# A graph layer on one Trainium2 core: layer 2 two blocks back and layer 1 one block back in each step, the adds directly behind the turns

## The chip, the core and the metric

The kernel runs on one core of a Trainium2 chip. The metric is the device time of one execution in microseconds (us). TensorE (PE), VectorE (DVE), ScalarE (ACT), GpSimd (POOL) and the queue of SyncE (SP), which issues DMA transfers, each run their own instructions in order and meet at semaphores.

## What is computed

```python
agg = jax.ops.segment_sum(edge_attr, dst, num_segments=6250)   # 106250 edges x 128, sorted by dst
h   = jnp.maximum(_layernorm(x, axis=-1), 0.0)                 # 6250 nodes x 128
y   = jax.nn.relu(jnp.concatenate([agg, h], axis=1) @ W1 + b1) # 256 -> 512
out = x + y @ W2 + b2                                          # 512 -> 128
```

All in float32. `src` isn't used. Each node has 17 edges on average, and the edges come sorted by their receiving node.

## The kernel before

**Tiling.** Nodes go in NB = 25 blocks of 256 (the last has 106). Edges go in rounds of 1536 (four chunks of 384), 70 rounds with the short last one; a block takes 4 (block 0), 3, or 2 (blocks 4, 10, 16 and 22) rounds, the last block takes the short one. Edge rounds land in a ring of eight slots. For each chunk DVE builds a one-hot matrix (`build`, L411) of each edge's node against a window of 32 nodes that begins at the chunk's first node, and TensorE multiplies it with the edges (`sum_rounds`, L666), which gives the sums of a window. ScalarE copies a block's sums from PSUM (`copy_sums`, L332), TensorE turns them (`turn_sums`, L677), and DVE adds each window into the node table `aggT` (`add_sums`, L481), at a place that it loads into registers from `base_tab` (L469).

**The node side.** DVE's `stats` (L424, L429), POOL's `spread` (L274 to L281) and ScalarE's `normalise` (L317) make the normalised rows `xn`; TensorE turns them (`turn_x`, L687); ScalarE rounds them into a high part (`h_out`, L324) and DVE keeps the rest as a low part (`rest_of_h`, L445). The aggregate is split in the same way by `round_agg` (ScalarE, L339) and `rest_of_agg` (DVE, L452). `layer1` (L703) has 24 products for a block, six for each quarter of the hidden units; ScalarE's `relu` (L350) brings the four quarters to SBUF, `layer2` (L715) multiplies them by W2, DVE's `finish` (L463) adds the residual with b2 (put in by `add_b2`, L438), and SP stores the block (`store`, L227).

**The order** is written out by hand: every engine runs a loop over the steps k = 0 to 24, and step k has work of several blocks. On TensorE a step is: sums of block k, layer 1 of block k-2, layer 2 of block k-3, turn of the sums of block k, turn of x of block k+1. On DVE: finish of k-4, adds of k-1, low part of h of k, one-hots of k+1, low part of the aggregate of k-1, statistics of k+2, b2 of k+1, and in steps 2, 3, 4, 5 and 7 parts of a check on whether the windows hold all edges (`overrun`, L499 to L507, and L567 to L577). On ScalarE: high part of h of k, copy of the sums of k, rounding of the aggregate of k-1, relu of k-2, normalise k+2. On SP: load of x of k+3, for each round of block k (once it is summed) a load of the round eight further, store of k-4.

Buffers that the order has to respect: one PSUM bank each for the sums, their turn, the turn of x and the output; two for the hidden units; two buffers each of `sums`, `xn`, `agg_hi`/`agg_lo`, `hidden` and `outrow`.

Of the kernel before, what the change touches and what calls it, by code (L numbers as in the profile page):

```python
# [26 lines left out]
def graph_layer(nc, x, dst, edge_attr, W1, b1, W2, b2, out):  # L27
# [40 lines left out]
    with ExitStack() as ctx:  # L68
# [137 lines left out]
        @block.sync  # L206
        def _(sp):
            def load(r):
                if r >= RING:
                    sp.wait_ge(round_summed, r - RING + 1)  # L210
                slot = r % RING
                if r == NR:
                    sp.dma_start(edges[0:KREST, slot, 0:GR * F], rest_v).then_inc(edges_landed[slot], 16)
                else:
                    sp.dma_start(edges[:, slot, :].rearrange("p (t n) -> p t n", t=TILES),  # L215
                                 rounds_v[:, r, :, :]).then_inc(edges_landed[slot], 16)

            def load_x(b):
                if b - 3 >= 4:
                    sp.wait_ge(x_landed[b % 4], 16 * ((b - 3) // 4))  # L220
                sp.dma_start(xs[:, b, :], x_v[:, b, :]).then_inc(x_landed[b % 4], 16)

            def store(n, par, b):
                sp.wait_ge(out_added, n + 1)
                w = width(b)
                if w == P:
                    sp.dma_start(out_v[:, bass.ds(b, 1), :], outrow[:, par:par + 1, :]).then_inc(stored[par], 16)  # L227
                else:
                    sp.dma_start(out_last_v, outrow[0:w, par, :]).then_inc(stored[par], 16)

            sp.dma_start(dstA[:, :], dst[0:P * CHUNK].rearrange("(c e) -> c e", e=CHUNK)).then_inc(dst_landed[0], 16)
            load(0)
            sp.dma_start(dstB[:, :], dst[P * CHUNK:2 * P * CHUNK].rearrange("(c e) -> c e", e=CHUNK)  # L233
                         ).then_inc(dst_landed[1], 16)
            sp.dma_start(dstC[:, :], dst[2 * P * CHUNK:FULL * CHUNK].rearrange("(c e) -> c e", e=CHUNK)  # L235
                         ).then_inc(dst_landed[2], 16)
            sp.dma_start(dstD[:, :], dst[FULL * CHUNK:E].rearrange("(a e) -> a e", a=1)).then_inc(dst_landed[3], 16)
            for r in range(1, RING):
                load(r)
            for k in range(NB):  # L240
                if 3 <= k + 3 < NB - 1:
                    load_x(k + 3)
                for r in ROUNDS[k]:
                    if r + RING < NROUNDS:
                        load(r + RING)
                if k >= 4:
                    store(k - 4, (k - 4) % 2, k - 4)
            for b in range(NB - 4, NB):
                store(b, b % 2, b)

            sp.wait_ge(stored[0], 16 * (NB // 2 + 1))
            sp.wait_ge(stored[1], 16 * (NB // 2))

            sp.wait_ge(flag_ready, 1)
            again = sp.value_load(flag[0:1, 0:1], min_val=0, max_val=1)
            with sp.If(again > 0):
                with sp.Fori(0, FULL) as c:
                    sp.wait_ge(wide_summed, c * NWIDE + 1)
                    sp.dma_start(edges[:, 0:1, 0:G * F], chunks_v[:, bass.ds(c, 1), :]).then_inc(wide_landed, 16)
                sp.wait_ge(wide_summed, FULL * NWIDE + 1)  # L260
                sp.dma_start(edges[0:KREST, 0, 0:GR * F], rest_v).then_inc(wide_landed, 16)
                with sp.Fori(0, NB - 1) as b:
                    store(NB + b, 0, b)
                store(2 * NB - 1, 0, NB - 1)
                sp.wait_ge(stored[0], 16 * (NB // 2 + 1 + NB))
# [37 lines left out]
        def _(act):  # L303
# [17 lines left out]
            def h_out(b):  # L321
                w = width(b)
                act.wait_ge(h_turned, b + 1)
                nc.scalar.activation(hT_hi[:, b * BLOCK:b * BLOCK + 2 * w], tr_ps[:, 0:2 * w],  # L324
                                     ACT.Copy).then_inc(hT_hi_ready, 1)
# [33 lines left out]
            nc.scalar.activation(w1_hi[:, :, :], w1[:, :, :], ACT.Copy).then_inc(w1_hi_ready, 1)  # L359
            for k in range(NB):  # L360
                h_out(k)
                copy_sums(k)
                if k == 0:
                    act.wait_ge(rel_turned, 3)
                    act.wait_ge(rel_copied, 5)
                    nc.scalar.activation(b1_col[:, :], misc_ps[:, 96:96 + HT], ACT.Copy).then_inc(b1_ready, 1)
                    act.wait_ge(b1_ready, 1)
                if k >= 1:
                    round_agg(k - 1, (k - 1) % 2, k - 1, chunks_by(k - 1))
                if k >= 2:  # L370
                    relu(k - 2, (k - 2) % 2, k - 2)
                if k + 2 < NB:
                    normalise(k + 2)
            relu(NB - 2, (NB - 2) % 2, NB - 2)
            round_agg(NB - 1, (NB - 1) % 2, NB - 1, FULL + 1)
            relu(NB - 1, (NB - 1) % 2, NB - 1)

# [15 lines left out]
        def _(dve):  # L393
# [70 lines left out]
                                        xs[0:w, bass.ds(b, 1), :].rearrange("p b f -> p (b f)"),  # L464
                                        ALU.add).then_inc(out_added, 1)

            def add_sums(k):
                first, last = (chunks_by(k - 1) if k else 0), chunks_by(k)
                _, bases = nc.values_load_multi_w_load_instructions(  # L469
                    base_tab[0:1, first:last], engines=[dve.engine], min_val=0, max_val=N - 1,  # L470
                    skip_runtime_bounds_check_because="clamped when written")
                dve.wait_ge(sums_turned, k + 1)
                if k:
                    dve.wait_ge(agg_added, first)
                order = list(range(first, last, 2)) + list(range(first + 1, last, 2))
                for n, c in enumerate(order):
                    if c == first + 1:
                        dve.wait_ge(agg_added, first + n)
                    win = aggT[:, bass.ds(bases[c - first], W)]
                    at = (c - first) * W  # L480
                    nc.vector.tensor_tensor(win, turn_ps[:, at:at + W], win, ALU.add).then_inc(agg_added, 1)  # L481
# [43 lines left out]
                                    ALU.subtract).then_inc(w1_ready, 1)  # L525

            for k in range(NB):
                if k >= 4:
                    finish(k - 4, (k - 4) % 2, k - 4)
                if k >= 1:  # L530
                    if k == 1:
                        dve.wait_ge(agg_cleared, CLEARS)
                    add_sums(k - 1)
                rest_of_h(k)
                if k == 0:
                    dve.wait_ge(rel_turned, 2)
                    turned_ab(1, rel_copied)
                    dve.wait_ge(rel_turned, 3)
                    turned_cd(rel_copied)
                    dve.wait_ge(bases_turned, 1)  # L540
                    nc.vector.tensor_scalar(base_tab[:, 0:FULL], row_ps[0:1, 0:FULL], 0.0, float(N - 1), ALU.max,
                                            ALU.min).then_inc(bases_ready, 1)
                    nc.vector.tensor_scalar(base_tab[:, FULL:FULL + 1], colD[:, 0:1], 0.0, float(N - 1), ALU.max,
                                            ALU.min).then_inc(bases_ready, 1)
                    add_b2(0)
                    dve.wait_ge(rel_copied, 5)
                    dve.wait_ge(bases_ready, 2)
                if k + 1 < NB:
                    for r in ROUNDS[k + 1]:
                        build(r)  # L550
                if k >= 1:
                    rest_of_agg(k - 1, (k - 1) % 2, k - 1)
                if k + 2 < NB:
                    stats(k + 2)
                if k + 1 < NB:
# [15 lines left out]
                if k == 7:  # L571
# [3 lines left out]
                    link(nc.vector.tensor_copy(over[:, 1:2], colD[:, 5:6]))  # L575
                    link(nc.vector.tensor_reduce(colD[:, 6:7], over[:, :], AX_X, ALU.max))
                    nc.vector.tensor_scalar(flag[:, :], colD[:, 6:7], 0.0, None, ALU.is_gt).then_inc(flag_ready, 1)  # L577
            finish(NB - 4, (NB - 4) % 2, NB - 4)
            add_sums(NB - 1)
            finish(NB - 3, (NB - 3) % 2, NB - 3)  # L580
            rest_of_agg(NB - 1, (NB - 1) % 2, NB - 1)
            finish(NB - 2, (NB - 2) % 2, NB - 2)
            finish(NB - 1, (NB - 1) % 2, NB - 1)
# [47 lines left out]
        def _(pe):  # L631
# [91 lines left out]
            for k in range(NB):  # L723
# [7 lines left out]
                    turn_cd().then_inc(rel_turned, 1)  # L731
                    turn_columns(0).then_inc(bases_turned, 1)
                if k == 2:
                    pe.wait_ge(w1_ready, 1)
                    pe.wait_ge(rel_copied, 5)
                if k >= 2:
                    layer1(k - 2, (k - 2) % 2, k - 2)
                if k == 3:
                    pe.wait_ge(w2_landed, 16)
                if k >= 3:  # L740
                    layer2(k - 3, (k - 3) % 2, k - 3)
                turn_sums(k)
                if k + 1 < NB:
                    turn_x(k + 1)
                if k == 6:
                    pe.wait_ge(overrun_ready, 4)
                    pe.wait_ge(bases_ready, 1)
                    turn_columns(5).then_inc(overrun_turned, 1)
            layer1(NB - 2, (NB - 2) % 2, NB - 2)
            layer2(NB - 3, (NB - 3) % 2, NB - 3)  # L750
            layer2(NB - 2, (NB - 2) % 2, NB - 2)
            layer1(NB - 1, (NB - 1) % 2, NB - 1)
            layer2(NB - 1, (NB - 1) % 2, NB - 1)
# [54 lines left out]
```

## Time and profile before

| | us |
|---|---|
| median of 3 runs | 219.34 (218.92 to 219.66) |
| the profiled execution: its own time | 219.65 |
| its span, first to last instruction | 217.9 |
| matmuls on TensorE (PE) | 195.5 busy, 90% |
| weight loads on TensorE (PEld) | 181.6 busy, 83% |
| DVE, ScalarE, POOL | 132.7 (61%), 92.9 (43%), 43.4 (20%) busy |
| DMA | 62.57 MB, mean 287 GB/s |

A row of groups or of the timeline has start, duration, engine, line, operation, out<-in and count; what stands in brackets is the idle time before it and what ended it. Where a row has several instructions, its duration runs from the first one's start to the last one's end. The end of a matmul is modelled. A step of the chain of waits is what the end of the program hung on at that time. TensorE's granted clock is given as a share of its full speed.

### The profile page before, as it was taken

The numbers are of one execution on the slowest core, as the hardware profiler recorded it, in microseconds if no ns is written. First come the engines' busy times: TensorE is split into PE (matmuls) and PEld (weight loads), VectorE is DVE, ScalarE is ACT, GpSimd is POOL, SyncE is SP. The second block draws the span as 40 slices with busy tenths as digits, with TensorE's granted clock in tenths as the row PEclk, the third lists the DMA queues.
The fourth block names the chain that finished last, engine by engine and source line by source line (L and its number), as shares of the span: only waits on it lengthen the run. The fifth ranks groups of instructions, "written<-read, shape, count | busy, mean of one in ns | idle before, by whom it ended". The sixth has DMA issues, their size and how long they took to land.

```text
span 217.9 us, 7403 instructions
## 1 busy us (share of the span) xinstructions
PE 195.5 (90%) x2813; PEld 181.6 (83%) x2813; DVE 132.7 (61%) x590; ACT 92.9 (43%) x229; POOL 43.4 (20%) x120
## 2 busy tenths in 40 slices
PE   1326959999999999999999999999999999999990
PEld 0214749999999999999999999999999999999880
DVE  2532777788888886477656764775578458531110
ACT  2230034454343664545445445455545464533320
POOL 4464012220222102222022022211220221100000
PEclk9999988999999999999999999999999999999997
DMA  6999999999999999998999999989999910000100
GB/s 212 296 371 371 376 374 377 377 377 375 380 383 384 385 385 373 380 367 277 333 382 342 328 346 375 354 255 346 379 339 346 347 32 24 27 24 20 34 24 13
DMA packets 44768, 62.57 MB, mean 287 GB/s; under 512 B 1939, under 2 KB 44438, under 8 KB 44732
## 3 DMA queue, kind: packets, MB, share of 16 engines
q1 hardware_dynamic: 43326, 60.78, 80.0%
q10 hardware_dynamic: 1406, 1.30, 1.9%
q8 instruction: 23, 0.38, 0.7%
q14 instruction: 13, 0.11, 0.1%
HBM read 58.88 MB, written 3.20 MB: 285 GB/s over the span
## 4 chain that ended last, share of the span: by engine, by line
PE 85%; DMA 7%; DVE 2%; issue 2%; SPq 1%; DVEq 0%
PE bank L703 35%; PE bank L666 21%; PE bank L715 21%; DMA edges<-in_edge_attr 7%; PE bank L677 4%; PE bank L687 2%; PE bank L659 1%; DVE aggT L481 1%; DVE onehot L411 1%; SPq L215 1%; DVE outrow L463 0%; PE bank L634 0%; SPq L233 0%; PE bank L645 0%; SPq L235 0%
## 5 line engine op out<-in xcount | busy, mean ns | idle before, releaser
L666 PE MATMUL bank<-edges,onehot 128*32 128x128 f32 x1656 | 55.7, 290 | 6.2 <-DMA edges<-in_edge_attr 6.2
L666 PEld LDWEIGHTS bank<-edges,onehot 128*32 128x32 f32 x1656 | 47.3, 117 | 12.4 <-DMA edges<-in_edge_attr 7.6
L350 ACT ACTIVATE hidden<-bank,b_col 128x256 f32<-128x256 f32 (+1 forms) x100 | 41.0, 466 | 30.6 <-PE bank L703 30.5
L715 PE MATMUL bank<-w,hidden 128*128 128x128 f32 (+1 forms) x400 | 48.9, 275 | 0.5 <-DVE outrow L463 0.5
L481 DVE TENSOR_TENSOR aggT<-bank,aggT 128x32 f32 x277 | 36.5, 192 | 20.0 <-issue 16.7
L715 PEld LDWEIGHTS bank<-w,hidden 128*128 128x128 f32 (+1 forms) x400 | 46.5, 189 | 1.0 <-DVE outrow L463 0.7
L317 ACT ACTIVATE xn<-xs,shift,rstd 128x128 f32<-128x128 f32 (+1 forms) x50 | 22.0, 486 | 44.5 <-POOL shift L281 44.5
L463 DVE TENSOR_TENSOR outrow<-bank,xs 128x256 f32<-128x256 f32 (+1 forms) x25 | 10.6, 424 | 40.3 <-PE bank L715 40.3
L274 POOL TENSOR_SCALAR var<-meanvar 128x2 f32<-128x2 f32 (+1 forms) x25 | 7.4, 297 | 135.8 <-DVE meanvar L429 135.8
L411 DVE TENSOR_TENSOR onehot<-relT,iota 128x384 f32<-128x384 f32 x69 | 34.3, 550 | 0.3 <-ACT iota L355 0.3
L703 PE MATMUL bank<-hT_hi,w_hi 128*128 128x256 f32 (+1 forms) x100 | 30.7, 307 | 0.0
L703 PE MATMUL bank<-agg_lo,w_hi 128*128 128x256 f32 (+1 forms) x100 | 28.5, 285 | 0.0
L703 PE MATMUL bank<-hT_lo,w_hi 128*128 128x256 f32 (+1 forms) x100 | 28.3, 283 | 0.0
L703 PE MATMUL bank<-agg_hi,w_lo 128*128 128x256 f32 (+1 forms) x100 | 28.1, 281 | 0.0
L703 PE MATMUL bank<-agg_hi,w_hi 128*128 128x256 f32 (+1 forms) x100 | 27.9, 279 | 0.0
L703 PE MATMUL bank<-hT_hi,w_lo 128*128 128x256 f32 (+1 forms) x100 | 27.8, 278 | 0.0
L332 ACT ACTIVATE sums<-bank 128x384 f32<-128x384 f32 (+3 forms) x25 | 11.6, 465 | 26.3 <-PE bank L666 24.9
L703 PEld LDWEIGHTS bank<-hT_hi,w_hi 128*128 128x128 f32 x100 | 18.8, 188 | 4.6 <-issue 4.6
L703 PEld LDWEIGHTS bank<-hT_lo,w_hi 128*128 128x128 f32 x100 | 19.0, 190 | 0.0
L703 PEld LDWEIGHTS bank<-hT_hi,w_lo 128*128 128x128 f32 x100 | 19.0, 190 | 0.0
L703 PEld LDWEIGHTS bank<-agg_hi,w_lo 128*128 128x128 f32 x100 | 18.8, 188 | 0.0
L703 PEld LDWEIGHTS bank<-agg_hi,w_hi 128*128 128x128 f32 x100 | 18.8, 188 | 0.0
(90 smaller groups left out, 189.1 us busy)
## 6 DMA issues: line engine op xcount, KB each, us to landing
edges<-in_edge_attr SPq DMA_DIRECT2D x69, 768.0 KB, 9.0
out_rows<-outrow SPq DMA_DIRECT2D x24, 128.0 KB, 8.5
xs<-in_x SPq DMA_DIRECT2D x21, 128.0 KB, 8.1
w<-in_L_gnn_W ACTq DMA_DIRECT2D x1, 512.0 KB, 6.6
xs<-in_x ACTq DMA_DIRECT2D x1, 384.0 KB, 3.9
hidden<-in_dst SPq DMA_DIRECT2D x2, 192.0 KB, 5.8
w<-in_L_gnn_W ACTq DMA_DIRECT2D x1, 256.0 KB, 10.2
edges<-in_edge_attr SPq DMA_DIRECT2D x1, 133.0 KB
```

Of the source, the lines that this page charges most:

```text
L274: nc.gpsimd.tensor_scalar(var[0:w, par, :], meanvar[0:w, par, :, 1], 1e-5, None, ALU.add).then_inc(var_ready, 1)
L317: ins = nc.scalar.activation(xn[0:w, par, j, :], xs[0:w, b, j * F:(j + 1) * F], ACT.Relu, bias=shift[0:w, par, j:j + 1], scale=rstd[0:w, p ...
L332: nc.scalar.activation(sums[0:rows, k % 2, 0:n], sums_ps[0:rows, 0:n], ACT.Copy).then_inc(sums_copied, 1)
L350: nc.scalar.activation(hidden[par][:, t, 0:2 * w], hid_ps[t // 2][:, (t % 2) * 2 * w:(t % 2 + 1) * 2 * w], ACT.Relu, bias=b1_col[:, t:t + ...
L411: nc.vector.tensor_tensor(hot, of.unsqueeze(2).to_broadcast([p, n, W]), iota[0:p, 0:W].unsqueeze(1).to_broadcast([p, n, W]), ALU.is_equal) ...
L463: nc.vector.tensor_tensor(outrow[0:w, par, :], out_ps[0:w, 0:2 * F], xs[0:w, bass.ds(b, 1), :].rearrange("p b f -> p (b f)"), ALU.add).the ...
L481: nc.vector.tensor_tensor(win, turn_ps[:, at:at + W], win, ALU.add).then_inc(agg_added, 1)
L666: ins = nc.tensor.matmul(sums_ps[t * W:(t + 1) * W, cols], onehot[:, hots, e, :], edges[:, slot, e * F:(e + 1) * F], start=(g == 0), stop= ...
L677: ins = nc.tensor.transpose(turn_ps[:, i * F:i * F + rows], sums[0:rows, k % 2, i * F:(i + 1) * F], ident[0:rows, 0:rows])
L687: ins = nc.tensor.transpose(tr_ps[:, j * w:(j + 1) * w], xn[0:w, par, j, :], ident[0:w, 0:w])
L703: ins = nc.tensor.matmul(o, wt[:, half, cols], v, start=(i == 0), stop=(i == 5))
L715: ins = nc.tensor.matmul(out_ps[0:w, j * F:(j + 1) * F], hidden[par][:, t, j * w:(j + 1) * w], w2[:, t, :], start=(t == 0), stop=(t == HT ...
```

## The change

No instruction is added or taken away. In step k TensorE now has: sums of block k, **layer 2 of block k-2**, the two turns, **layer 1 of block k-1**. On ScalarE the rounding of the aggregate of k-1 stands ahead of the copy of the sums of k, and the relu is that of block k-1 and comes last, behind normalise. On DVE the low part of the aggregate comes ahead of the one-hots, and the step ends with: loading the windows' places, finish of k-2, adds of k (before, the adds of k-1 came in step k, behind finish of k-4). SP stores block k-3 in step k.

```diff
-                if k >= 4:
-                    store(k - 4, (k - 4) % 2, k - 4)
-            for b in range(NB - 4, NB):
+                if k >= 3:
+                    store(k - 3, (k - 3) % 2, k - 3)
+            for b in range(NB - 3, NB):
                 store(b, b % 2, b)
...
             for k in range(NB):
                 h_out(k)
+                if k >= 1:
+                    round_agg(k - 1, (k - 1) % 2, k - 1, chunks_by(k - 1))
                 copy_sums(k)
...
-                if k >= 1:
-                    round_agg(k - 1, (k - 1) % 2, k - 1, chunks_by(k - 1))
-                if k >= 2:
-                    relu(k - 2, (k - 2) % 2, k - 2)
                 if k + 2 < NB:
                     normalise(k + 2)
-            relu(NB - 2, (NB - 2) % 2, NB - 2)
+                if k >= 1:
+                    relu(k - 1, (k - 1) % 2, k - 1)
...
             for k in range(NB):
-                if k >= 4:
-                    finish(k - 4, (k - 4) % 2, k - 4)
-                if k >= 1:
-                    if k == 1:
-                        dve.wait_ge(agg_cleared, CLEARS)
-                    add_sums(k - 1)
                 rest_of_h(k)
...
+                if k >= 1:
+                    rest_of_agg(k - 1, (k - 1) % 2, k - 1)
                 if k + 1 < NB:
                     for r in ROUNDS[k + 1]:
                         build(r)
-                if k >= 1:
-                    rest_of_agg(k - 1, (k - 1) % 2, k - 1)
...
-            finish(NB - 4, (NB - 4) % 2, NB - 4)
-            add_sums(NB - 1)
-            finish(NB - 3, (NB - 3) % 2, NB - 3)
+                bases = load_bases(k)
+                if k >= 2:
+                    finish(k - 2, (k - 2) % 2, k - 2)
+                if k == 0:
+                    dve.wait_ge(agg_cleared, CLEARS)
+                add_sums(k, bases)
...
                 if k == 2:
-                    pe.wait_ge(w1_ready, 1)
-                    pe.wait_ge(rel_copied, 5)
+                    pe.wait_ge(w2_landed, 16)
                 if k >= 2:
-                    layer1(k - 2, (k - 2) % 2, k - 2)
-                if k == 3:
-                    pe.wait_ge(w2_landed, 16)
-                if k >= 3:
-                    layer2(k - 3, (k - 3) % 2, k - 3)
+                    layer2(k - 2, (k - 2) % 2, k - 2)
                 turn_sums(k)
                 if k + 1 < NB:
                     turn_x(k + 1)
...
-            layer1(NB - 2, (NB - 2) % 2, NB - 2)
-            layer2(NB - 3, (NB - 3) % 2, NB - 3)
+                if k == 1:
+                    pe.wait_ge(w1_ready, 1)
+                    pe.wait_ge(rel_copied, 5)
+                if k >= 1:
+                    layer1(k - 1, (k - 1) % 2, k - 1)
             layer2(NB - 2, (NB - 2) % 2, NB - 2)
```

ScalarE, steps 1 and 2, from the turn of x of block 1 on (`agg_hi` is the aggregate's high part, `hidden` the relu's output), before:

```order
L324 ACTIVATE hT_hi<-bank 128x256
L332 ACTIVATE sums<-bank 128x384
L339 ACTIVATE agg_hi<-aggT 128x256
L317 ACTIVATE xn<-xs,shift,rstd 128x128 x2
L324 ACTIVATE hT_hi<-bank 128x256
L332 ACTIVATE sums<-bank 128x384
L339 ACTIVATE agg_hi<-aggT 128x256
L350 ACTIVATE hidden<-bank,b_col 128x256 x4
L317 ACTIVATE xn<-xs,shift,rstd 128x128 x2
```

and with the change:

```order
L324 ACTIVATE hT_hi<-bank 128x256
L339 ACTIVATE agg_hi<-aggT 128x256
L332 ACTIVATE sums<-bank 128x384
L317 ACTIVATE xn<-xs,shift,rstd 128x128 x2
L350 ACTIVATE hidden<-bank,b_col 128x256 x4
L324 ACTIVATE hT_hi<-bank 128x256
L339 ACTIVATE agg_hi<-aggT 128x256
L332 ACTIVATE sums<-bank 128x384
L317 ACTIVATE xn<-xs,shift,rstd 128x128 x2
L350 ACTIVATE hidden<-bank,b_col 128x256 x4
```

The copy of the sums went behind the rounding, and the relu behind normalise, a step earlier than it was.

TensorE, the end of step 1, all of step 2 and the start of step 3. Before:

```order
L677 MATMUL bank<-ident,sums 128x128 x3
L687 MATMUL bank<-ident,xn 128x128 x2
L666 MATMUL bank<-edges,onehot 32x128 x36
L703 MATMUL bank<-hT_hi,w_hi 128x256
...
L703 MATMUL bank<-agg_hi,w_lo 128x256
L677 MATMUL bank<-ident,sums 128x128 x3
L687 MATMUL bank<-ident,xn 128x128 x2
L666 MATMUL bank<-edges,onehot 32x128 x36
```

and with the change:

```order
L677 MATMUL bank<-ident,sums 128x128 x3
L687 MATMUL bank<-ident,xn 128x128 x2
L703 MATMUL bank<-hT_hi,w_hi 128x256
...
L703 MATMUL bank<-agg_hi,w_lo 128x256
L666 MATMUL bank<-edges,onehot 32x128 x36
L715 MATMUL bank<-w,hidden 128x128 x8
L677 MATMUL bank<-ident,sums 128x128 x3
L687 MATMUL bank<-ident,xn 128x128 x2
```

Layer 1 of block 0 (24 products) now comes ahead of the sums of block 2, and layer 2 of block 0 comes a step earlier, between sums and turns.

## Rows read from the trace of the kernel before

**Rows 1.** Who TensorE waited for: us in total, times, longest

```profile
PE bank L666 <- DMA edges<-in_edge_attr: 6.2, 3, 3.5
PE bank L677 <- DVE aggT L481: 2.3, 1, 2.3
```

**Rows 2.** Chain that ended last, a step of three rounds, then sums of two

```profile
149.20 2.10 PE bank L666 x72
151.30 3.06 PE bank L703 x24
154.37 1.78 PE bank L715 x16
156.15 0.33 PE bank L677 x3
156.48 0.22 PE bank L687 x2
...
179.19 1.45 PE bank L666 x48
```

**Rows 3.** Timeline, all engines, around the adds of block 0

```profile
29.45 0.48 ACT L332 ACTIVATE sums<-bank 128x384 f32<-128x384 f32 x1
29.62 0.90 DVE L481 TENSOR_TENSOR aggT<-bank,aggT 128x32 f32 x7 [0.36 <-issue]
...
30.55 0.44 ACT L339 ACTIVATE agg_hi<-aggT 128x256 fp32r<-128x256 f32 x1 [0.62 <-DVE aggT L481]
...
30.66 0.73 PE L677 MATMUL bank<-ident,sums 128*128 128x128 f32 x3 [2.33 <-DVE aggT L481]
```

**Rows 4.** Stretches of 1 us, TensorE: length, PE busy, clock share, DMA, GB/s

```profile
30.00:31.00 1.00, 0.34 (x3) 0.91 1.07 375
...
34.00:35.00 1.00, 1.00 (x36) 0.88 1.06 387
```

**Rows 5.** Timeline of DVE in steps 5 to 7

```profile
54.22 0.53 DVE L499 TENSOR_REDUCE colC<-relC 20x1 f32<-20x384 f32 x1
...
57.13 0.43 DVE L463 TENSOR_TENSOR outrow<-bank,xs 128x256 f32<-128x256 f32 x1
58.05 1.22 DVE L481 TENSOR_TENSOR aggT<-bank,aggT 128x32 f32 x8 [0.49 <-issue]
...
63.41 0.42 DVE L463 TENSOR_TENSOR outrow<-bank,xs 128x256 f32<-128x256 f32 x1
...
66.10 0.41 DVE L445 TENSOR_TENSOR hT_lo<-bank,hT_hi 128x256 fp32r<-128x256 f32 x1
...
68.75 0.25 DVE L429 BATCH_NORM_AGGREGATE meanvar<-halves 128x2 f32<-128x6 f32 x2
...
69.23 0.42 DVE L463 TENSOR_TENSOR outrow<-bank,xs 128x256 f32<-128x256 f32 x1
```

**Rows 6.** Timeline of ScalarE in steps 3 and 7

```profile
44.17 1.56 ACT L350 ACTIVATE hidden<-bank,b_col 128x256 f32<-128x256 f32 x4
...
70.80 0.88 ACT L317 ACTIVATE xn<-xs,shift,rstd 128x128 f32<-128x128 f32 x2 [2.67 <-POOL shift L281]
71.58 0.36 ACT L324 ACTIVATE hT_hi<-bank 128x256 fp32r<-128x256 f32 x1
```

**Rows 7.** Timeline, all engines, the last layers

```profile
203.22 0.84 ACT L350 ACTIVATE hidden<-bank,b_col 128x256 f32<-128x256 f32 x2 [0.59 <-PE bank L703]
...
205.00 0.42 DVE L463 TENSOR_TENSOR outrow<-bank,xs 128x256 f32<-128x256 f32 x1 [4.29 <-PE bank L715]
...
205.48 2.05 PE L715 MATMUL bank<-w,hidden 128*128 128x128 f32 x16 [0.52 <-DVE outrow L463]
```

**Rows 8.** Transfers that read the tile outrow

```profile
DMA to landing us min/median/max: 1.7/8.5/10.3
```

**Rows 9.** Line L279, the power on POOL: ns min/median/max, first and last start

```profile
L279 POOL TENSOR_TENSOR rstd<-var,power x25: 702/709/875, 6.2 to 185.0; 128x2 f32<-128x2 f32 x24, 53x2 f32<-53x2 f32 x1
```

More of the change, by code:

```diff
@@ L465, in finish, with load_bases @@
                                         ALU.add).then_inc(out_added, 1)
-            def add_sums(k):
+            def load_bases(k):
                 first, last = (chunks_by(k - 1) if k else 0), chunks_by(k)
@@ L471, in add_sums @@
                     skip_runtime_bounds_check_because="clamped when written")
+                return bases
+            def add_sums(k, bases):
+                first, last = (chunks_by(k - 1) if k else 0), chunks_by(k)
                 dve.wait_ge(sums_turned, k + 1)
```

## The prediction

> **What bounds the kernel now.** I read the waits of TensorE first: the largest are 6.2 us for edges, all before 20 us, and 2.3 us in front of the turn of a block's sums, at 28.3 to 30.7 [rows 1, 3]. Behind that only 0.5 us is left, at 205 [rows 7]. In between the chain of waits is one unbroken row of TensorE work: a step is 2.10 (sums) + 3.06 (layer 1) + 1.78 (layer 2) + 0.33 + 0.22 (turns) = 7.49 us [rows 2], and no other engine appears in it. So an order of the same work can move the time only in three places: where TensorE starts to run without a gap, where its tail has a gap, and where the new order makes a gap that was not there. Nothing is removed or added: counts per engine are the same.
>
> **The start.** Up to the adds of block 0 both programs have the same order on every engine. Those adds end at 29.62 + 0.90 = 30.52 us [rows 3]. Before, the copy of block 1's sums (L332) was done at 29.45 + 0.48 = 29.93, so the turn L677 started at 30.66, behind the adds alone. Now ScalarE has the rounding of block 0's aggregate (L339, waits for those adds) ahead of that copy. L339 starts at 30.55 and takes 0.44; an activation begins some 0.08 to 0.1 before the end of the one ahead of it, as L324 at 71.58 does behind xn [rows 6], so the copy starts at 30.91 and with its 0.48 ends at 31.39. With the 0.07 to 0.1 us that a hand-over takes here (30.52 to 30.63), the turn starts at 31.45 instead of 30.66: **+0.8 us**. Layer 1 of block 0 follows at once (its low part is ready at 31.05 + 0.4 = 31.45 on DVE), and the sums of block 2 behind it find their one-hots built; so +0.8 is the whole shift.
>
> The clock softens this. The granted share is 0.91 over the slice 30 to 31 and 0.88 over 34 to 35, and it was 0.50 between [rows 4]: TensorE, idle for 2.3 us, fell to the lower level (1.2 of 2.4 GHz) at about 30.9 and rose again at about 34.3. If fall and rise stay where they are, the later restart spends 0.8 us less of the slow stretch working, at half speed: -0.4 us. If the stretch moves along with the restart, 0. The stretch began while TensorE was idle, so I take the first: start = **+0.4**, bounds +0.4 and +0.8. A second slow stretch of the same 3.4 us would cost 1.7 more; it is part of the upper range.
>
> **The steps.** I put t = 0 at the start of a step's sums. TensorE: sums to 2.10, layer 2 to 3.88, turns to 4.43, layer 1 to 7.49. What must be ready, with the durations of [rows 5, 6]:
> - ScalarE applies the second half of layer 1's relu behind layer 1 (0.07 + 0.84 us, as at 203.22 [rows 7]): done at 8.4, which is 0.9 of the next step. Layer 2 of that block wants it at 2.10: margin 1.2.
> - The turn of h's block (L324) follows on ScalarE at 0.8, DVE's L445 0.39 later (0.36 and a hand-over of 0.03), then L339 and DVE's L452, done by 2.1. Layer 1 wants it at 4.43: margin 2.3.
> - The copy of the sums is done at 2.10 + 0.5 = 2.6 and wanted at 3.88.
> - DVE from L445 to the end of the statistics takes 69.00 - 66.10 = 2.90 us whatever the order of the four items in it, so they end at 4.1; finish follows behind layer 2 and the adds end near 6.9. Next needed: 8.3.
>
> The narrow place is a **ring through four engines**. The relu now stands behind normalise, which waits for POOL, which waits for DVE's statistics, which wait for L324, which stands behind the previous relu. Its length: L324 to L445 0.39, DVE 2.90, statistics to xn 1.80 (69.00 to 70.80), xn to the next activation 0.78 (70.80 to 71.58), four relus 1.46 (1.56 less the 0.1 by which the next one overlaps). Sum 7.33 us against TensorE's 7.49. It fits, by 0.16 us. With only two rounds in a block both get shorter by 0.5 to 0.7. I therefore put the steady steps at **0**.
>
> DVE's own round is 69.23 - 63.41 = 5.82 us a step [rows 5], 1.67 less than TensorE's. In step 4 it has 57.13 - 54.22 = 2.91 us of overrun checks besides, now ahead of finish and the adds. With layer 1 of block 0 from 32.5 to 36.8 (most of it at the slow clock), the sums of blocks 2 to 6 start at 36.8, 44.3, 51.8, 58.5 (behind a step of two rounds) and 66.0. In step 4 L324 starts at 52.6, the statistics end at 55.9 (two rounds built in step 3, three here), L438 lets go at 56.1, the checks at 59.1, loading eight window bases takes 58.05 - 57.13 - 0.34 = 0.58, finish 0.34, eight adds 1.2: they end at 61.2. L339 and the copy of block 5's sums are done at 62.1. TensorE comes out of block 5's sums at 60.6 and out of layer 2 of block 3 at 62.4, and wants the copy there: margin 0.3. The next statistics end 3.1 us behind those adds, at 64.3; xn starts at 66.1, the relus of block 4 at 66.9, and the fourth is done at 68.5. Layer 2 starts at 68.1 and its fourth product wants it at 68.8: margin 0.3 again. Then the ring gains 0.16 a step. I take **0**, with bounds 0 and 1.6, the 2.91 less the spare 1.3 us between adds (6.9) and L445 (8.2 to 8.7) of a quiet step.
>
> The junctions of TensorE's work are new: sums to layer 2, turns to layer 1, layer 1 to sums. In [rows 2] a change into or out of the sums costs some 0.1 us of exposed weight load each way (72 records of sums take 2.10 where 48 take 1.45, so 1.95 and 0.15 for the edges), and both changes stay, one in and one out per step. I take 0; bounds 0.1 us either way in each of 22 steps, so -2.2 and +2.2.
>
> The queues: SP's store of a block moves one step forward and its loads wait for the sums of blocks that now run some 5 us later. A store lands 8.5 us after its issue, at most 10.3 [rows 8]. Store k-4 is issued at about 2.6 of step k-1 and finish k-2, the first to reuse that buffer, comes at 4.9 of step k: 9.8 us later. A landing of 10.3 delays finish by 0.5, and the adds have 1.4 to spare. Loads are eight rounds ahead, 20 us, and land in 9. Cost 0. The later sums also mean that SP waits more for TensorE and less for full queues; nobody waits for that.
>
> POOL: the page "GPSIMD Engine Reference" of the Trainium skill (section Specifications) says that GpSimd shares its interfaces to SBUF with VectorE and contends with DVE instructions that have two SBUF inputs. Here L438 is one, and it runs into POOL's first small operation in both orders. The power on POOL takes 702 to 875 ns, 709 in the middle [rows 9], so the trace shows 0.17 us at most. By that rule the ring could be 7.5 rather than 7.33; by the rows it is not, and the sum goes by the rows.
>
> **The tail.** Before, layer 2 of block 23 followed that of block 22 and waited for its finish: 205.00 to 205.48 [rows 7], 0.48 us. Now layer 1 of block 23 lies in front of it, so finish 22 is long done; but its own relu is not. Two products fill 0.45 us, the third relu is ready after 0.07 + 0.47 and the fourth after 0.91, where the products want them at 0.45 and 0.67: 0.26 us lost with the hand-over. -0.48 + 0.26 = **-0.2**. The last layer 1 wants L452 of block 24, ready 1.4 us after layer 1 of block 23, and gets there after 2.0.
>
> **Sum.** +0.4 + 0 + 0 - 0.2 = +0.2 us on the profiled execution's own 219.65: 219.85, say **219.9**. That execution stands 0.3 above the median of the runs shown, 219.34. I keep 219.9 for the median too: a run that escapes the slow stretch is what I suspect behind the lowest, 218.92, and a gap of 3.1 us instead of 2.3 makes that rarer.
>
> **The rivals.** A measurement of this kernel can tell 0.3%, 0.66 us, from no change.
> - *The checks in step 4 open a gap* (other side: slower). Finish and adds of block 4 behind 2.91 us of checks, then L339, then the copy, then TensorE. It decides as soon as the chain is 0.3 us longer than I summed. Price up to 1.6: 219.9 + 1.6 = 221.5, in the middle 220.7. For it: two margins of 0.3 built from some fifteen durations. Against: 1.67 us of slack a step.
> - *The ring is longer than TensorE's step* (slower). From 7.49 on it decides; at 7.65 it costs 0.16 in each of some 18 steps: 2.9 us, 222.8. The skill's rule on shared interfaces would be such a cause. Against it: each piece was read while DVE and POOL ran side by side.
> - *The junctions are cheaper* (faster): layer 2 right behind the sums loads its weights under them. 0.1 x 22 = 2.2: 217.7. The rows give no sign, since the load is exposed at every entry to and exit from the sums.
> - *Nothing to be seen*: start and tail cancel: 219.3 to 219.6. It is the low end of my own case.
>
> **How the numbers follow.** My forecast, steps without a gap and 219.3 to 220.4: 0.62, of which two thirds stay within 0.66 us of the median. Gap in steps 4 to 6: 0.2. Ring: 0.1. Junctions faster: 0.08. So faster 0.08, within 0.3% 0.50, slower 0.42. The range leaves out the cheap junctions and most of the long ring: 219.1 to 221.8.
>
> **What would show it.** Right: TensorE's first turn after the idle gap starts at 31.4 to 31.5; the chain has steps of 7.49 without a wait; layer 2 of block 23 shows a short wait for L350 and none for L463; ScalarE's xn waits for POOL less than now. Wrong: waits of TensorE for L332 or L350 near 62 and 68 us (first rival), waits for L350 in many steps and a step over 7.5 (second), a step under 7.45 (third), or TensorE waiting for edges.

## The result and the profile after

The changed kernel takes 220.82 us in the median of 12 runs (220.37 to 222.27), the kernel before 219.27 (218.78 to 219.66, 12 runs beside them): a ratio of 1.0074, 95% interval 1.0056 to 1.0091. It is slower by 1.55 us, inside the range, and more than the 0.6 us that was forecast. The profiled execution took 220.76 us with a span of 219.0, against 219.65 and 217.9 before: 1.1 us more. Where that 1.1 us lies can be read from the two traces. Of all the runs in this document one is left out of a median and a ratio: a run of the kernel before with ten added matmuls took 291.22 us at a mean granted share of 0.684.

TensorE's waits in the changed kernel, us in total, times, longest (before: [rows 1]):

```profile
PE bank L666 <- DMA edges<-in_edge_attr: 6.1, 3, 3.3
...
PE bank L677 <- ACT sums L332: 3.0, 1, 3.0
PE bank L715 <- DVE outrow L462: 0.4, 1, 0.4
```

The turn now waits for ScalarE's copy and not for the adds. And the wait of layer 2 for finish is there still, but no longer at the end: it is at 60 us.

**Start.** The timeline around the adds of block 0, where [rows 3] stand before:

```profile
29.90 0.43 DVE L484 TENSOR_TENSOR aggT<-bank,aggT 128x32 f32 x3
30.25 0.41 DVE L444 TENSOR_TENSOR hT_lo<-bank,hT_hi 128x256 fp32r<-128x256 f32 x1
30.36 0.43 ACT L339 ACTIVATE agg_hi<-aggT 128x256 fp32r<-128x256 f32 x1 [1.05 <-DVE aggT L484]
30.70 0.47 ACT L332 ACTIVATE sums<-bank 128x384 f32<-128x384 f32 x1
...
31.23 0.69 PE L677 MATMUL bank<-ident,sums 128*128 128x128 f32 x2 [2.95 <-ACT sums L332]
```

The adds end at 29.90 + 0.43 = 30.33 us, 0.2 earlier than before, and the turn starts 0.90 us behind them, where it was 0.14: a shift of 0.76 us against the 0.8 that was summed. The clock's slices of 1 us answer to [rows 4]:

```profile
30.00:31.00 1.00, 0.00 (x0) 0.97 1.07 378
34.00:35.00 1.00, 1.00 (x9) 0.83 1.06 389
```

With 0.97 and 0.83 the lower level reaches from some 30.9 to 34.3, as before. It stayed where it was and TensorE worked less of it, but by 0.2 us and not by 0.4, since TensorE also began 0.2 us earlier than I had put it.

**A step** of three rounds in the chain of waits, in the new order (before: [rows 2]):

```profile
149.64 1.98 PE bank L715 x16
151.62 0.33 PE bank L677 x3
151.95 0.22 PE bank L687 x2
152.17 2.86 PE bank L703 x24
155.03 2.10 PE bank L666 x72
```

1.98 + 0.33 + 0.22 + 2.86 + 2.10 = 7.49 us, the sum of before. Layer 2 has 0.2 more and layer 1 has 0.2 less: what the engine loses on the way out of the sums now stands in front of layer 2. The junctions cost the same.

**Block 3, at 60 us.** Here the chain leaves TensorE:

```profile
58.91 0.15 DVE colD L505
...
59.27 0.15 DVE colD L510
59.41 0.47 DVEq L468
...
60.03 0.43 DVE outrow L462
60.47 0.04 issue
60.51 2.05 PE bank L715 x16
```

Checks, loading of the windows' places, finish of block 2, and only then layer 2 of block 3. The sums of block 5 take 2.61 us from their first product to the next line's, where other steps have 2.10: a gap of 0.51. In layer 2 of block 3, in the turns behind it and in the next layer 2 another 0.14 us go. Together 0.65 us.

DVE was not made late by step 4 alone. Between the adds of block 0 and 60.51 us this chain holds no instruction of TensorE. After one pass over POOL and ScalarE in step 1 it runs in a loop over the low part of the aggregate, one-hots, statistics, b2, checks, loading of the places, adds, and ScalarE's rounding in between, and the checks of steps 2 and 3 are in it as well:

```profile
41.04 0.47 DVE colA L502
...
42.69 0.70 DVEq L468
...
48.35 0.47 DVE colB L502
...
49.99 0.71 DVEq L468
```

The low part of the aggregate (L451) starts at 38.16, 45.94, 53.63 and 62.03 us, so DVE's rounds of steps 2, 3 and 4 take 7.78, 7.69 and 8.40 us. The sums start at 36.17, 43.67, 51.17 and 57.90, so TensorE has steps of 7.50, 7.50 and 6.73 us there.

**Tail**, as the chain has it:

```profile
203.08 0.17 PE bank L677
203.25 3.09 PE bank L703 x24
206.34 0.02 issue
206.36 0.48 ACT hidden L350
...
206.89 1.75 PE bank L715 x12
208.64 2.62 PE bank L703 x24
211.26 1.99 PE bank L715 x16
```

Layer 2 waits for its own relu, and not for a finish as in [rows 7]. From the turn at 203.08 to the end of the last layer 2 at 213.25 it is 10.17 us. Before, the same stretch took 12.20 us (199.94 to 212.14) with one layer 2 (1.78) more in it, so 10.42 without. The tail gains 0.25 us.

So the profiled execution has -0.2 (adds earlier) + 0.76 - 0.2 (clock) + 0.65 - 0.25 = +0.8 of its +1.1. Of the other 0.3 us some 0.2 lie in step 6, where three turns of the checks now stand between the turn of x and layer 1; the rest I can't place. This is TensorE's own account. It does not say that the start, put back alone, would return its part, since the chain at 60 us comes from DVE.

### The profile page after: what moved, and what is told of

The parts are those of the page before. It is cut to its first block, busy times and chain, and to the rows that moved or that the text cites. A ratio compares the mean times of both kernels' runs of the same rounds, so it can differ in the third digit from the quotient of the medians.

```text
span 219.0 us, 7403 instructions
## 1 busy us (share of the span) xinstructions
PE 196.2 (90%) x2813; PEld 182.6 (83%) x2813; DVE 131.2 (60%) x590; ACT 87.8 (40%) x229; POOL 43.4 (20%) x120
## 4 chain that ended last, share of the span: by engine, by line
PE 71%; DVE 11%; DMA 7%; issue 3%; ACT 2%; SPq 1%; DVEq 1%; POOL 1%; POOLq 0%
PE bank L703 28%; PE bank L715 20%; PE bank L666 17%; DMA edges<-in_edge_attr 7%; DVE onehot L410 3%; PE bank L677 3%; PE bank L687 2%; DVE aggT L484 2%; DVE halves L423 1%; DVEq L468 1%; ACT hidden L350 1%; PE bank L659 1%; DVE agg_lo L451 1%; SPq L215 1%; ACT agg_hi L339 1%
## 5 line engine op out<-in xcount | busy, mean ns | idle before, releaser
L666 PE MATMUL bank<-edges,onehot 128*32 128x128 f32 x1656 | 54.7, 287 | 6.1 <-DMA edges<-in_edge_attr 6.1
L666 PEld LDWEIGHTS bank<-edges,onehot 128*32 128x32 f32 x1656 | 46.5, 115 | 11.6 <-DMA edges<-in_edge_attr 7.8
L715 PE MATMUL bank<-w,hidden 128*128 128x128 f32 (+1 forms) x400 | 51.7, 282 | 0.6 <-DVE outrow L462 0.4
L350 ACT ACTIVATE hidden<-bank,b_col 128x256 f32<-128x256 f32 (+1 forms) x100 | 38.7, 458 | 12.7 <-PE bank L703 12.7
L484 DVE TENSOR_TENSOR aggT<-bank,aggT 128x32 f32 x277 | 34.4, 187 | 6.3 <-issue 2.2
L274 POOL TENSOR_SCALAR var<-meanvar 128x2 f32<-128x2 f32 (+1 forms) x25 | 7.4, 296 | 140.6 <-DVE meanvar L428 140.6
L410 DVE TENSOR_TENSOR onehot<-relT,iota 128x384 f32<-128x384 f32 x69 | 34.3, 551 | 0.5 <-ACT iota L355 0.5
L444 DVE TENSOR_TENSOR hT_lo<-bank,hT_hi 128x256 fp32r<-128x256 f32 (+1 forms) x25 | 10.4, 416 | 33.0 <-ACT hT_hi L324 33.0
L703 PEld LDWEIGHTS bank<-agg_lo,w_hi 128*128 128x128 f32 x100 | 19.0, 190 | 0.0
```

Of the source, the lines that this page charges most:

```text
L274: nc.gpsimd.tensor_scalar(var[0:w, par, :], meanvar[0:w, par, :, 1], 1e-5, None, ALU.add).then_inc(var_ready, 1)
L350: nc.scalar.activation(hidden[par][:, t, 0:2 * w], hid_ps[t // 2][:, (t % 2) * 2 * w:(t % 2 + 1) * 2 * w], ACT.Relu, bias=b1_col[:, t:t + ...
L410: nc.vector.tensor_tensor(hot, of.unsqueeze(2).to_broadcast([p, n, W]), iota[0:p, 0:W].unsqueeze(1).to_broadcast([p, n, W]), ALU.is_equal) ...
L444: nc.vector.tensor_tensor(hT_lo[:, cols], tr_ps[:, 0:2 * w], hT_hi[:, cols].bitcast(F32), ALU.subtract).then_inc(hT_lo_ready, 1)
L666: ins = nc.tensor.matmul(sums_ps[t * W:(t + 1) * W, cols], onehot[:, hots, e, :], edges[:, slot, e * F:(e + 1) * F], start=(g == 0), stop= ...
L703: ins = nc.tensor.matmul(o, wt[:, half, cols], v, start=(i == 0), stop=(i == 5))
```

## The experiments

The theory after reading the traces: the start costs a copy (0.76 less what the clock gives back), the checks cost 0.65, everything else is level. Rivals: the ring through POOL and the relu, or the junctions. Four kernels undo parts of the change. In all diffs lines are those of the changed kernel.

**Copy first, in step 1 alone**

```diff
                 h_out(k)
+                if k == 1:
+                    copy_sums(k)
                 if k >= 1:
                     round_agg(k - 1, (k - 1) % 2, k - 1, chunks_by(k - 1))
-                copy_sums(k)
+                if k != 1:
+                    copy_sums(k)
```

> The changed kernel (220.8 us) with one thing put back: in step 1 alone the copy of the sums (L332) stands ahead of the rounding of the aggregate (L339) again. Theory (the start costs a copy behind the adds): the first turn starts some 0.1 us behind the adds again and not 0.9, TensorE works 0.75 us more of the slow stretch at half speed, so 0.75 less 0.4 comes back: 220.4 to 220.5. But TensorE then reaches block 5 some 0.4 us earlier, where DVE is not earlier, and if the gap in front of layer 2 of block 3 hangs on DVE alone it grows by what the start gained: then 220.8 as before. Rival (the start is nothing, the time is in the gap at 60 us): 220.8 too, but with the gap unchanged at 0.5. The trace tells the two apart.

Measured: 221.0 us (220.5 to 221.19), ratio 1.0075 (1.0055 to 1.0094). Nothing is won. Two of the waits of its TensorE:

```profile
PE bank L680 <- DVE aggT L487: 1.6, 1, 1.6
PE bank L718 <- DVE outrow L465: 0.7, 1, 0.7
```

The turn waits for the adds again, and the wait for finish has grown from 0.4 to 0.7. From the first product of block 5's sums to layer 2 it is 2.88 us and not 2.61, so the gap grew from 0.51 to 0.78 us. DVE reaches block 3 when it does, and a TensorE that comes earlier waits longer. In the profiled execution the slow stretch also fell later, onto layer 1 of block 0 in full (granted share 0.50 from 31.95 to 35.36 us).

**Checks later**

```diff
-                if k == 2:
+                if k == 10:
                     dve.wait_ge(limit_ready, 1)
                     overrun(colA, relA, limit[:, 0:1])
-                if k == 3:
+                if k == 12:
                     overrun(colB, relB, limit[:, 1:2])
-                if k == 4:
+                if k == 14:
                     overrun(colC, relC, limit[0:CC, 2:3])
+                if k == 16:
                     overrun(colD, relD, None)
-                if k == 5:
+                if k == 17:
...
-                if k == 7:
+                if k == 19:
...
-                if k == 6:
+                if k == 17:
                     pe.wait_ge(overrun_ready, 4)
```

> The changed kernel with the checks of the windows moved from steps 2, 3, 4, 5, 7 to 10, 12, 14, 16, 17, 19, the last two parts apart. Theory (the gap in front of layer 2 of block 3 and the small ones behind it, 0.65 us in the trace, come from the checks that stand ahead of finish and adds): no wait of TensorE for L462 near 60 us, 220.2. Rival (the ring DVE, POOL, ScalarE is too long by itself): the gap comes a few steps later and the time stays at 220.8.

Measured: 220.2 us (218.65 to 220.47), ratio 1.0023 (1.0000 to 1.0046). These are all the waits of its TensorE:

```profile
PE bank L667 <- DMA edges<-in_edge_attr: 6.2, 3, 3.4
PE bank L635 <- DVE relA L489: 4.1, 1, 4.1
PE bank L688 <- ACT xn L317: 3.3, 1, 3.3
PE bank L678 <- ACT sums L332: 2.6, 1, 2.6
```

No wait for finish is left, and none came up later. The checks cost 0.6 us.

**Both edits**

> Both edits. Theory: start and gap add up, 220.8 - 0.65 - 0.4 = 219.8, or 0.3 less if the tail's gain shows; within 0.5 of the kernel before. If it stays over 220.5, something else than start and gap makes the new order slower (junctions of TensorE's work).

Measured: 219.6 us (218.36 to 220.26, 12 runs), ratio 1.0003 (0.9985 to 1.0021): level with the kernel before. With the gap gone, the start seems worth the 0.6 us that it wasn't worth alone: that is the difference of the two medians, and the intervals of the two ratios, 1.0000 to 1.0046 and 0.9985 to 1.0021, overlap. Together the two parts account for all of the measured loss. The profiled execution, 220.26 us, is the longest of the twelve, and its clock shows why (length of the slice, PE busy, granted share, DMA):

```profile
29.00:30.00 1.00, 0.00 (x0) 0.66 1.06 373
30.00:31.00 1.00, 0.90 (x5) 0.50 1.06 372
...
35.00:36.00 1.00, 1.00 (x7) 0.50 1.06 375
36.00:37.00 1.00, 1.00 (x27) 0.92 1.09 382
```

Here TensorE ran at the lower level for 6.8 us and not 3.4, though it was busy from 30.1 on.

**Finish ahead of the checks, in step 4 alone**

```diff
                 if k == 4:
+                    finish(k - 2, (k - 2) % 2, k - 2)
                     overrun(colC, relC, limit[0:CC, 2:3])
...
-                if k >= 2:
+                if k >= 2 and k != 4:
                     finish(k - 2, (k - 2) % 2, k - 2)
```

> The changed kernel, in step 4 alone finish of block 2 ahead of the checks; the adds stay behind them. Theory A (TensorE waits for finish, and nothing stands close behind): the gap at 60 us goes, 220.3. Theory B (the adds and the copy of block 5's sums are nearly as late): the gap of 0.5 is replaced by one of 0.1 to 0.4 in front of the turn of block 5's sums, 220.5 to 220.7.

Measured: 221.4 us (220.87 to 222.33), ratio 1.0105 (1.0081 to 1.0128). Theory B, and more than it said; three of the six runs, 221.54 to 222.33 us, have a mean granted share of 0.979 to 0.980, the others 0.990 to 0.995. TensorE and DVE there:

```profile
59.75 2.05 PE L716 MATMUL bank<-w,hidden 128*128 128x128 f32 x16
62.39 0.44 PE L678 MATMUL bank<-ident,sums 128*128 128x128 f32 x2 [0.59 <-ACT sums L332]
```

```profile
59.45 0.15 DVE L510 SCALAR_TENSOR_TENSOR colD<-colD 1x1 f32<-1x1 f32 x1
60.28 1.22 DVE L484 TENSOR_TENSOR aggT<-bank,aggT 128x32 f32 x8 [0.68 <-issue]
```

Layer 2 starts at once, but the turn behind it waits 0.59 us for the copy and starts at 62.39, where it started at 62.42. The adds start at 60.28 and not at 60.37, but DVE's statistics (L428) ended 0.31 us earlier in this execution; from there to the adds it takes 0.22 us longer. From L510 to the first add it is 0.83 us, and 1.10 with finish in between, so there finish costs 0.27 us. Ahead of the checks it costs 0.50: from the start of b2 (L437) to that of the first check (L502) it is 0.81 us, and 0.31 without it. So two hand-overs lay within a few tenths of each other, finish to layer 2 and adds to copy to turn, and both hang on the checks.

**The slow stretch.** Ten matmuls that nothing reads fill TensorE's idle time, in the kernel before and in the changed one with both edits:

```diff
                 turn_sums(k)
...
+                if k == 1:
+                    for i in range(10):
+                        nc.tensor.matmul(out_ps[:, 0:F], ident[:, :], ident[:, :], start=True, stop=True)
                 turn_sums(k)
```

> The kernel before with ten 128x128 matmuls of the identity with itself into the output's bank, behind the sums of block 1, where TensorE has nothing to do for 2.3 us; nothing reads them. Theory (the slow stretch at 31 to 34 us comes from that idle time and costs what the trace shows, 1.6 us): the granted share stays at 1.0 and the time falls from 219.3 to 217.7. Rival (the clock falls anyway, or the time is won back nowhere because another engine is just as late): 219.3.

Measured: 218.84 us (218.09 to 219.62, 11 runs) against 219.27, ratio 0.9987 (0.9973 to 1.0001). That is a quarter of what was expected, and the interval still holds no change. The clock stays at 1.00 in all slices from 28 to 34 us, but a new wait appears:

```profile
38.66 0.86 PE L666 MATMUL bank<-edges,onehot 128*32 128x128 f32 x24 [0.25 <-DMA edges<-in_edge_attr]
```

In the order of before the sums of block 3 now run ahead of their edges; the sums of that block take 0.46 us longer. The old order needs the edges early, and DMA already moved 370 to 375 GB/s in the slices from 28 to 34 us. That is 0.5 of the missing 1.2 us. The profiled execution itself is 1.1 us shorter than that of before (218.52 against 219.65), as theory and edge wait together would have it.

The runs of the kernel before say that 1.6 us was too high a price for the median. A full stretch of 3.41 us at half clock takes 3.41 / 2 / 217.9 = 0.008 off the mean granted share. Of the 55 runs of before that were taken beside the experiments, six have a share of 0.998 or 0.999 and so had no such stretch. Their median is 219.05 us, that of the other 49, with 0.981 to 0.992, is 219.35. So the old order gains some 0.3 us when the stretch stays away, whether or not the ten matmuls see to it. With both edits in the new order it is more: the two runs with a share of 0.993, which is too high for a full stretch, took 218.36 and 218.39 us, the other ten 219.05 to 220.26. Why the old order gains only 0.3 is not shown beyond the edge wait.

> The changed kernel with copy first in step 1, checks later, and the same ten matmuls. Theory: 219.8 - 1.5 = 218.3, or a bit less. With layer 1 of block 0 at full speed TensorE comes 1.4 us earlier to every later block while DVE, POOL and ScalarE are not earlier; if the ring then binds, part of it is lost in the steps behind: 218.3 to 219.5.

Measured: 218.47 us (218.24 to 218.83), ratio 0.9965 (0.9953 to 0.9978), faster than the kernel before. Layer 1 and layer 2 of block 0 now stand between the sums of blocks 1, 2 and 3, and TensorE's waits behind 22 us hold none for edges. It loses 0.33 us in front of layer 2 of block 0, where the relu waits for xn.

**The ring.** One more operation of 0.47 us on DVE in each step from 8 on, in both kernels:

```diff
+                if k >= 8:
+                    nc.vector.tensor_tensor(relA[:, :].rearrange("p (e w) -> p e w", w=W),
...
                 if k + 2 < NB:
                     stats(k + 2)
```

> The kernel before with one more DVE operation of 0.47 us in each step from 8 on, ahead of the statistics; it writes a tile that only the branch for windows that hold not all edges would read, and that branch isn't taken. DVE's round is 5.82 + 0.47 = 6.29 us against TensorE's 7.49: 219.3, no change.

Measured: 219.29 us against 219.27, ratio 1.0000 (0.9986 to 1.0013). No change.

> The changed kernel with the same operation. If the ring L324, DVE, POOL, xn, relu, L324 is 7.33 us long, it is 7.80 now, and over the 16 steps it falls 5.8 us behind TensorE's own pace, of which 1 us is spare: 225 to 226, with waits for L350 or L317 in most steps. If the ring isn't closed (DVE's load alone counts, 6.29 us a step): 220.8.

Measured: 225.57 us (225.02 to 226.51), ratio 1.0302 (1.0279 to 1.0325), 4.8 us over the changed kernel, as the ring has it. ScalarE's timeline in it shows the ring turn:

```profile
103.63 0.88 ACT L317 ACTIVATE xn<-xs,shift,rstd 128x128 f32<-128x128 f32 x2 [4.61 <-POOL shift L281]
104.42 1.54 ACT L350 ACTIVATE hidden<-bank,b_col 128x256 f32<-128x256 f32 x4
105.84 0.39 ACT L324 ACTIVATE hT_hi<-bank 128x256 fp32r<-128x256 f32 x1
...
113.65 0.39 ACT L324 ACTIVATE hT_hi<-bank 128x256 fp32r<-128x256 f32 x1
...
121.45 0.39 ACT L324 ACTIVATE hT_hi<-bank 128x256 fp32r<-128x256 f32 x1
```

L324 follows L324 after 7.81 and 7.80 us: 7.33 + 0.47. The relu has no idle time in front of it, it follows xn directly, and xn waits 4.6 us for POOL. In its trace layer 2 takes 0.3 us more in nearly every step.

The same kernel, with the relu ahead of normalise:

```diff
+                if k >= 1:
+                    relu(k - 1, (k - 1) % 2, k - 1)
                 if k + 2 < NB:
                     normalise(k + 2)
-                if k >= 1:
-                    relu(k - 1, (k - 1) % 2, k - 1)
```

> The changed kernel with the additional DVE operation of 0.47 us in each step from 8 on, as in the run before (225.6 us), but on ScalarE the relu of block k-1 stands ahead of normalise k+2. The operation writes a tile that only the branch not taken would read. Theory (the ring runs through xn and relu): the relu no longer waits for POOL, the ring is L324, DVE, POOL, xn, L324 and 1.46 us shorter, 6.3 us with the operation, and nothing is lost from it: 220.8, or up to 0.5 less. Rival (DVE's load or its hand-overs as such): 225.6 again.

Measured: 221.78 us (219.64 to 222.5), ratio 1.0122 (1.0097 to 1.0148). 3.8 of the 4.8 us are gone: the ring ran through xn and relu. ScalarE now waits for TensorE and not for POOL. The wait for POOL is 12.3 us in all, where the changed kernel has 94.0:

```profile
ACT hidden L350 <- PE bank L707: 94.4, 50, 3.7
ACT xn L317 <- POOL shift L281: 12.3, 3, 5.7
```

**The relu ahead of normalise, alone**

> The changed kernel with the relu ahead of normalise, nothing else. The gap in front of layer 2 of block 3 hangs on DVE's checks and finish. L324 comes 0.8 us later in a quiet step, but in steps 3 and 4 xn was late itself. Theory: the checks still fall on the same place, 220.8, gap 0.3 to 0.6. If the gap goes, the ring had a share in it: the statistics of step 4 then end earlier: 220.2.

Measured: 221.28 us (219.79 to 221.77), ratio 1.0088 (1.0056 to 1.0119). The gap at 60 us grew to 0.9 us, more than I had expected at most. It is the same 0.9 in the run before, which explains the 1 us that stayed there. L324, now behind normalise too, starts at 37.70 us in step 2 and not at 37.40, DVE's L444 behind it at 38.10 and not at 37.82, and DVE's loop over the checks carries that on: finish of block 2 starts at 60.36 and not at 60.03. In steps 3 and 4 DVE no longer waits for L324. So the relu's place does not cure the gap; it trades the ring for a later DVE.

**All together:** copy first, checks later, ten matmuls, relu ahead of normalise.

> Copy first in step 1, checks later, ten matmuls in the idle time (218.5 us together), and the relu ahead of normalise. The 0.3 us that TensorE lost in front of layer 2 of block 0 at 36 us, where the relu waited for xn, go: 218.2. If normalise, now behind the relu, makes the next turn of x late: 218.5 or more.

Measured: 218.24 us (217.98 to 218.58), ratio 0.9954 (0.9935 to 0.9972): the fastest of all, 1.1 us under the kernel before (219.36 beside it). From the first turn to the tail TensorE waits for nobody; the start of its chain there:

```profile
28.74 2.48 PE bank L743 x20
31.22 0.33 PE bank L681 x3
31.55 0.22 PE bank L691 x2
31.77 2.87 PE bank L707 x24
34.64 2.10 PE bank L670 x72
36.74 1.98 PE bank L719 x16
```

L743 are the ten matmuls in the idle time (the trace has two records for each); layer 2 of block 0 follows the sums of block 2 without a gap.

## Why the prediction was right and wrong

- *TensorE bounds every step, and the order changes nothing in it.* Right: 7.49 us in both, junctions included.
- *Start +0.4, bounds 0.4 and 0.8.* The shift was 0.76 (0.8 summed), shown by the hand-over in the trace and by the pair of experiments (0.6 us between checks later alone and both edits). The clock gave back 0.2 and not 0.4, so the value lay between my bounds. My reason for the choice was misread: in [rows 3, 4] the share of 0.91 puts the fall at 30.8 us, and TensorE had begun again at 30.66, so the stretch did not begin while it was idle. That it stayed in its place in the profiled execution is luck as far as these runs show; in those of "copy first" and "both edits" it began at 31.95 and 29.32. And in the changed kernel as it stands the start is not on the chain of waits, since DVE's loop holds up layer 2 at 60 us either way.
- *Steps 4 to 6: 0, with two margins of 0.3 and a bound of 1.6.* This is the step that failed. The first rival came true, with 0.65 us, at less than its middle price. I had the end of the sums of block 5 at 60.6; it was 60.0, since TensorE started earlier and layer 1 was shorter. I had finish at 59.1 + 0.58 = 59.68; it was 60.03, since the statistics ended 0.3 later and the loading took 0.6. The statistics were late because I charged DVE with the checks of step 4 alone and gave it 1.67 us of slack in every other step. The checks of steps 2 and 3 stand ahead of the adds too, and with them DVE's rounds took 7.78 and 7.69 us and not 5.82. When step 4 began, L324 was done at 52.42 and DVE was still adding until 53.12. And the place was not the one I watched (adds, copy, turn) but finish to layer 2, for which I had noted no margin at all. By my own sum it would have been 0.4: finish from 59.68 for 0.43 and a hand-over of 0.05, against 60.6. Moving the checks removed it, moving finish only moved it. A margin of 0.3 us out of fifteen durations deserved a price, not a zero.
- *The ring is 7.33 us, 0.16 less than a step.* Right to 0.01: in the changed kernel, at 149 to 157 us, L324 to DVE's L444 takes 0.42, DVE 2.92, statistics to xn 1.78, xn to relu 0.79, relu to L324 1.42: 7.33. And with 0.47 more on DVE the step became 7.80. The second rival did not occur, but its mechanism is real and stands 0.16 us away. I had read POOL's part off its power (L279) alone, and that missed a cost. The power has its median at 707 ns here, 709 before and 709 in the kernel with the additional operation, but in the ring it never runs beside a DVE instruction that reads two tensors in SBUF. Beside the one-hots at 6 us it did, and took 1043 ns (875 before). POOL's first operation, L274, runs beside DVE's L437 in every step and takes 0.30 us; in the first and the last block, where it doesn't, it took 0.23 and 0.22. The page "GPSIMD Engine Reference" of the Trainium skill (section Specifications) has POOL contend with DVE's instructions that have two SBUF inputs, and the trace agrees: some 0.08 us a step, which the measured 1.78 and so the 7.33 already hold.
- *Tail -0.2.* Right: -0.25, and the new wait is for L350 as said.
- *Junctions cheaper.* Did not occur.
- *Edges and stores cost nothing.* Right; stores land after 8.2 us, at most 9.5.
- *Measured +1.55 us against +0.6.* Of the missing 0.95 the gap is 0.6 to 0.65. The remaining 0.3 is of the size of step 6 and the slow stretch, which varies from run to run.

## What to carry to other kernels

When the bounding engine already runs without a gap, a new order of the same work can only move its start and end or open gaps. Look for what it now lets stand in front of a hand-over: a copy behind an addition at the start, one-off work in front of a hand-over that had two steps of slack. Shorter distance between the stages closes rings over several engines; sum the ring against the step, because it does not show until a little is added to one of its parts. One-off work adds up in the same way: sum an engine's rounds over all the steps that hold some of it, and not only over the heaviest.

## What was not expected of the hardware

- TensorE's low clock is no steady price, neither in how long it lasts nor in what it costs: without it the median of before is 0.3 us lower, and that of the new order with both edits 1.3 us (two runs of twelve). It lasted 3.4 us in the profiled executions of both kernels, 6.8 us in that of "both edits" (granted share 0.50 from about 29.3 to 36.1 although TensorE was busy from 30.1 on), and did not come at all in that of the extra operation with the relu first, 219.64 us, where TensorE had been idle for 3.7 us, to 31.0 (granted share 1.00 throughout); the other four runs of that kernel took 221.6 to 222.5.
- In the changed kernel three of twelve runs took 221.7 to 222.3 us with a mean granted share of 0.98, the other nine 220.4 to 220.9 with 0.984 to 0.991. Whether those three had the long stretch is likely but wasn't seen, since only one execution of a kernel is traced.
- Loading window places into DVE's registers hides behind a waiting or running instruction only in part: with finish between loading and adds, finish cost 0.27 us, and ahead of the checks 0.50.
- POOL slows down beside DVE's one-hots. This happens in one block of the changed kernel, the first: there the power took 1043 ns (median 707) and L281, the product behind it, 334 (median 195).
